# The difference of two probabilities, in two tiles of four added up in PSUM by products with the identity

## The reference, cut to what matters

```python
def _prob(x):
    x = jnp.tanh(x) * 0.499 + 0.5
    return jnp.clip(x / (jnp.sum(x, axis=-1, keepdims=True) + EPS), EPS)
q_prob = _prob(q)
k_prob = _prob(k)
log_ratio = jnp.log(q_prob) - jnp.log(k_prob)
sid = jnp.einsum('bnd,bmd->bnm', q_prob - k_prob, log_ratio)
attn = jax.nn.softmax(-sid / D ** 0.5, axis=-1)
attn_feat = jnp.einsum('bnm,bmd->bnd', attn, v)
```

## Time and profile before

| | |
|---|---|
| median of 3 runs | 262.26 us (262.22 to 262.55) |
| the profiled execution | 262.99 us, span of its instructions 261.1 us |
| mean granted clock of TensorE | 0.933 |
| stage two | about 64 to 124 us of the span |
| busy over the span | VectorE 225.0 us, ScalarE 216.2, TensorE 209.4, GpSimd 188.9 |

### The profile page before, as it was taken

How to read it: one execution, slowest core, us unless ns; L and a number is a source line. 1 busy time by engine, 2 the same in 40 slices (tenths; PEclk the granted TensorE clock), 3 DMA queues, 4 the chain that set the end, 5 groups by cost and what they waited for, 6 DMA issues and landing times.

```text
span 261.1 us, 5925 instructions
## 1 busy us (share of the span) xinstructions
PE 209.4 (80%) x1723; PEld 176.3 (68%) x1723; DVE 225.0 (86%) x843; ACT 216.2 (83%) x774; POOL 188.9 (72%) x250
## 2 busy tenths in 40 slices
PE   2676676754499888887899999999999999996711
PEld 1664554533387666666689988888889888895600
DVE  2899999988879999999525889999999999999892
ACT  4599999998889999989997888988898887776521
POOL 2477666764899999991885796969697888666552
PEclk9999999795569999999999999999999999999765
DMA  5667554540000000000328189897978888977922
GB/s 140 188 201 204 158 154 135 154 113 1 1 0 3 0 3 3 1 3 4 40 32 91 12 100 135 122 133 110 151 115 132 129 125 128 137 121 121 103 61 61
DMA packets 51360, 23.65 MB, mean 91 GB/s; under 512 B 9856, under 2 KB 51200, under 8 KB 51328
## 3 DMA queue, kind: packets, MB, share of 16 engines
q0 software_dynamic: 15856, 7.87, 28.0%
q1 hardware_dynamic: 35040, 15.21, 21.9%
q10 hardware_dynamic: 432, 0.20, 0.4%
HBM read 9.37 MB, written 4.19 MB: 52 GB/s over the span
## 4 chain that ended last, share of the span: by engine, by line
POOL 28%; DVE 23%; ACT 20%; issue 13%; PE 11%; DMA 3%; SPq 0%; POOLq 0%; DVEq 0%; ACTq 0%
POOL F L407 7%; POOL xrstd L448 7%; ACT TQK L523 6%; ACT TQK L507 6%; POOL orstd L442 6%; DVE q_c L810 5%; POOL F L454 5%; DVE LN_c L818 5%; DVE F L838 5%; PE bank L1011 3%; ACT PV L518 3%; DMA LN_c<-in_ctx_dram 3%; ACT vT_c L512 2%; PE bank L960 1%; DVE F L863 1%
## 5 line engine op out<-in xcount | busy, mean ns | idle before, releaser
L1011 PE MATMUL bank<-W2T,TQK 128*128 128x128 f32 x512 | 68.7, 282 | 2.6 <-ACT TQK L545 2.5
L1011 PEld LDWEIGHTS bank<-W2T,TQK 128*128 128x128 f32 x512 | 64.0, 194 | 8.5 <-ACT TQK L545 4.0
L545 ACT ACTIVATE TQK<-bank,b1c 128x512 f32<-128x512 f32 (+1 forms) x68 | 44.5, 661 | 10.7 <-PE bank L1004 10.4
L448 POOL TENSOR_TENSOR xrstd<-xvar,pow_c 128x4 f32<-128x4 f32 (+1 forms) x17 | 18.5, 1090 | 23.2 <-DVE xvar L726 23.2
L362 POOL TENSOR_TENSOR xrstd<-xvar,pow_c 128x4 f32<-128x4 f32 x16 | 16.8, 1051 | 21.5 <-DVE xvar L726 21.5
L1002 PE MATMUL bank<-hTh,W1h 128*128 128x512 f32 (+1 forms) x68 | 30.4, 447 | 0.8 <-DVE hTl L801 0.8
L407 POOL DMA_DIRECT2D F<-rows x17 | 26.0, 1529 | 5.6 <-DVE E_c L796 5.6
L1003 PE MATMUL bank<-hTl,W1h 128*128 128x512 f32 (+1 forms) x68 | 26.1, 384 | 0.0
L1004 PE MATMUL bank<-hTh,W1l 128*128 128x512 f32 (+1 forms) x68 | 25.9, 382 | 0.0
L960 PE MATMUL bank<-WdT,vT_c 128*128 128x128 f32 x128 | 20.5, 309 | 4.8 <-ACT vT_c L512 4.6
L951 PE MATMUL bank<-ident,LN_c 128*128 128x128 f32 x64 | 12.3, 322 | 13.9 <-DMA LN_c<-in_ctx_dram 13.9
(11 more groups left out here) (129 smaller groups left out, 645.2 us busy)
## 6 DMA issues: line engine op xcount, KB each, us to landing
F<-rows POOLq DMA_DIRECT2D x29, 256.0 KB, 4.7
LN_c<-in_ctx_dram SPq DMA_DIRECT2D x16, 256.0 KB, 3.0
X<-in_x_dram SPq DMA_DIRECT2D x16, 256.0 KB, 3.3
out_dram<-F SPq DMA_DIRECT2D x15, 256.0 KB, 2.3
LN_c<-in_L_xattn_W_dram SPq DMA_DIRECT2D x1, 256.0 KB, 3.5
lT_c<-in_L_xattn_W_dram SPq DMA_DIRECT2D x1, 256.0 KB, 3.7
F<-rows POOLq DMA_DIRECT2D x2, 128.0 KB, 4.8
out_dram<-F SPq DMA_DIRECT2D x2, 128.0 KB, 1.8
```

The lines of the kernel that those rows point to most:

```text
L448: pool.tensor_tensor(buf(xrstd, x1, G), buf(xvar, x1, G), pow_c[:, 0:x1.g], ALU.pow).then_inc(x1_rstd, 1)
L545: act.activation(hid(m, j), m1_bank(m, j), ACT.Gelu, bias=b1c[:, j:j + 1]).then_inc(gelu_ready, 1)
L1011: last = pe.matmul(M2_B[m.buf][:, i * D:(i + 1) * D], hid(m, j)[:, i * D:(i + 1) * D], W2T[:, j * D:(j + 1) * D], start=(j == 0 and i == 0 ...
```

## The change

GpSimd makes k's part for all tiles of a piece and nothing else in this stage. ScalarE no longer makes k's parts; for the first half of a piece's tiles it scales q's tanh by GAINQ in place in TQ, after Ln has read it (`qparts`, behind Exp in the step). TensorE adds the two parts of those tiles in PSUM while it transposes them: a product of k's part with the identity, and a product of q's part with the identity accumulated onto it. VectorE makes the difference for the other half as before, and the log ratio for all tiles. D now waits for three semaphores: k's parts, q's parts, VectorE's differences. The waits on `kpart_act`, `diff_pool` and `lr_pool` are gone.

```diff
@@ gpsimd phase2
-                    for i in range(by_act(k), k.g):
-                        last = pool.tensor_scalar(tile(diff_c, k, i), all_tile(TK, k, i), per_tile(GAINK, k, i),
+                    for i in range(k.g):
+                        last = pool.tensor_scalar(tile(k_c, k, i), all_tile(TK, k, i), per_tile(GAINK, k, i),
                                                   per_tile(SHIFT, k, i), ALU.mult, ALU.add)
                     last.then_inc(kpart, 1)
-                    if k.g == G:
-                        i = G - 1
...
-                        pool.tensor_scalar(qpart_c, all_tile(TQ, k, i), per_tile(GAINQ, k, i), None,
-                                           ALU.mult).then_inc(qpart, 1)
...
-                        pool.tensor_tensor(tile(diff_c, k, i), qpart_c, tile(diff_c, k, i),
-                                           ALU.add).then_inc(diff_pool, 1)
...
-                        pool.tensor_scalar(ln_tile(0, k, i), ln_tile(0, k, i), per_tile(LRATIO, k, i), None,
-                                           ALU.add).then_inc(lnq_pool, 1)
...
-                        pool.tensor_tensor(ln_tile(1, k, i), ln_tile(0, k, i), ln_tile(1, k, i),
-                                           ALU.subtract).then_inc(lr_pool, 1)
@@ scalar
-            def kparts(k):
-                wait(act, dT_ps, k.n - 1)
-                if is_piece(k, NORMS):
-                    act.wait_ge(norms, 2)
+            def qparts(k):
+                act.wait_ge(ln_ready, k.n + 1)
                 for i in range(by_act(k)):
-                    last = act.activation(tile(diff_c, k, i), all_tile(TK, k, i), ACT.Identity,
-                                          bias=per_tile(SHIFT, k, i), scale=per_tile(GAINK, k, i))
-                last.then_inc(kpart_act, 1)
+                    last = act.activation(all_tile(TQ, k, i), all_tile(TQ, k, i), ACT.Copy, scale=per_tile(GAINQ, k, i))
+                last.then_inc(q_act, 1)
@@ scalar phase2, behind Exp
+                k0 = at(0)
+                if k0.live:
+                    if k0.n == 0:
+                        act.wait_ge(norms, 1)
+                    if k0.n == NORMS:
+                        act.wait_ge(norms, 2)
+                    qparts(k0)
@@ scalar phase2, behind the copies
-                k = at(-1)
-                if k.live:
-                    kparts(k)
@@ vector phase2
-                    for i in range(by_dve(k)):
-                        last = dve.scalar_tensor_tensor(out=tile(diff_c, k, i), in0=all_tile(TQ, k, i),
...
-                    last.then_inc(diff_ready, 1)
+                    for i in range(by_act(k), k.g):
+                        last = dve.scalar_tensor_tensor(out=tile(k_c, k, i), in0=all_tile(TQ, k, i),
...
+                    last.then_inc(diff_dve, 1)
...
-                    for i in range(by_dve(k)):
+                    for i in range(k.g):
                         last = dve.scalar_tensor_tensor(out=ln_tile(1, k, i), in0=ln_tile(0, k, i),
@@ tensor phase2
-                    pe.wait_ge(diff_ready, k.n + 1)
-                    pe.wait_ge(diff_pool, wholes(k.n + 1))
+                    pe.wait_ge(kpart, k.n + 1)
+                    pe.wait_ge(q_act, k.n + 1)
+                    pe.wait_ge(diff_dve, k.n + 1)
                     wait(pe, dT_sb, k.n)
-                    for i in range(k.g):
-                        last = pe.transpose(D_B[:, i * D:(i + 1) * D], tile(diff_c, k, i), ident[:, :])
+                    for i in range(by_act(k)):
+                        at_i = D_B[:, i * D:(i + 1) * D]
+                        pe.matmul(at_i, tile(k_c, k, i), ident[:, :], start=True, stop=False)
+                        pe.matmul(at_i, all_tile(TQ, k, i), ident[:, :], start=False, stop=True)
+                    for i in range(by_act(k), k.g):
+                        last = pe.transpose(D_B[:, i * D:(i + 1) * D], tile(k_c, k, i), ident[:, :])
```

More of the change, by code:

```diff
@@ L152, in xattn_ffn_kernel @@
         vT_c = sb("vT_c", [P, 2 * C])
-        diff_c, dT_c = q_c, vT_c
+        k_c, dT_c = q_c, vT_c
         lT_c = sb("lT_c", [P, 2 * C])
@@ L174, in xattn_ffn_kernel @@
         r16_c = LN_c[:, 2 * C:3 * C].bitcast(F16)
-        qpart_c = RNORM[:, :]
         Wd_raw = E_c[:, 0:D]
@@ L199, in by_act @@
             return k.g // 2
[L201 to L205, removed]
         def tile(t, k, i):
@@ L274, in xattn_ffn_kernel @@
         norm_step, halfk_ready, norms, lratio = sem("norm_step"), sem("halfk_ready"), sem("norms"), sem("lratio")
-        kpart, kpart_act, ln_ready, diff_ready, lr_ready = (
-            sem("kpart"), sem("kpart_act"), sem("ln_ready"), sem("diff_ready"), sem("lr_ready"))
-        qpart, diff_pool, lnq_pool, lr_pool = sem("qpart"), sem("diff_pool"), sem("lnq_pool"), sem("lr_pool")
+        kpart, ln_ready, q_act, diff_dve, lr_ready = (
+            sem("kpart"), sem("ln_ready"), sem("q_act"), sem("diff_dve"), sem("lr_ready"))
         dT_ps, dT_sb, lT_ps, lT_sb = sem("dT_ps"), sem("dT_sb"), sem("lT_ps"), sem("lT_sb")
@@ L378, in phase2 @@
                         pool.wait_ge(norms, 2)
-                    for i in range(by_act(k), k.g):
-                        last = pool.tensor_scalar(tile(diff_c, k, i), all_tile(TK, k, i), per_tile(GAINK, k, i),
+                    for i in range(k.g):
+                        last = pool.tensor_scalar(tile(k_c, k, i), all_tile(TK, k, i), per_tile(GAINK, k, i),
                                                   per_tile(SHIFT, k, i), ALU.mult, ALU.add)
                     last.then_inc(kpart, 1)
-                    if k.g == G:
-                        i = G - 1
-                        pool.wait_ge(kpart, k.n + 1)
-                        if is_piece(k, 0):
-                            pool.wait_ge(norms, 2)
-                        pool.tensor_scalar(qpart_c, all_tile(TQ, k, i), per_tile(GAINQ, k, i), None,
-                                           ALU.mult).then_inc(qpart, 1)
-                        pool.wait_ge(qpart, k.n + 1)
-                        pool.tensor_tensor(tile(diff_c, k, i), qpart_c, tile(diff_c, k, i),
-                                           ALU.add).then_inc(diff_pool, 1)
-                        pool.wait_ge(ln_ready, k.n + 1)
-                        if is_piece(k, 0):
-                            pool.wait_ge(lratio, 1)
-                        pool.tensor_scalar(ln_tile(0, k, i), ln_tile(0, k, i), per_tile(LRATIO, k, i), None,
-                                           ALU.add).then_inc(lnq_pool, 1)
-                        pool.wait_ge(lnq_pool, k.n + 1)
-                        pool.tensor_tensor(ln_tile(1, k, i), ln_tile(0, k, i), ln_tile(1, k, i),
-                                           ALU.subtract).then_inc(lr_pool, 1)
             pool.wait_ge(norms, 1)
@@ L566, in phase2 @@
                     wait(act, lr_ready, k.n - 1)
-                    wait(act, lr_pool, wholes(k.n - 1))
                     wait(act, lT_ps, k.n - 1)
@@ L615, in _ @@
             act.wait_ge(sel_ready, 1)
-            act.wait_ge(norms, 1)
-            kparts(pairs[0])
             run_steps(pairs, 2, phase2)
@@ L806, in phase2 @@
                 if k.live:
-                    dve.wait_ge(kpart_act, k.n + 1)
                     dve.wait_ge(kpart, k.n + 1)
-                    for i in range(by_dve(k)):
-                        last = dve.scalar_tensor_tensor(out=tile(diff_c, k, i), in0=all_tile(TQ, k, i),
-                                                        scalar=per_tile(GAINQ, k, i),
-                                                        in1=tile(diff_c, k, i), op0=ALU.mult, op1=ALU.add)
-                    last.then_inc(diff_ready, 1)
+                    for i in range(by_act(k), k.g):
+                        last = dve.scalar_tensor_tensor(out=tile(k_c, k, i), in0=all_tile(TQ, k, i),
+                                                        scalar=per_tile(GAINQ, k, i), in1=tile(k_c, k, i),
+                                                        op0=ALU.mult, op1=ALU.add)
+                    last.then_inc(diff_dve, 1)
                     dve.wait_ge(ln_ready, k.n + 1)
@@ L1051, in phase2 @@
                 if k.live:
-                    pe.wait_ge(diff_ready, k.n + 1)
-                    pe.wait_ge(diff_pool, wholes(k.n + 1))
+                    pe.wait_ge(kpart, k.n + 1)
+                    pe.wait_ge(q_act, k.n + 1)
+                    pe.wait_ge(diff_dve, k.n + 1)
                     wait(pe, dT_sb, k.n)
-                    for i in range(k.g):
-                        last = pe.transpose(D_B[:, i * D:(i + 1) * D], tile(diff_c, k, i), ident[:, :])
+                    for i in range(by_act(k)):
[4 more added lines that the diff above has]
+                        last = pe.transpose(D_B[:, i * D:(i + 1) * D], tile(k_c, k, i), ident[:, :])
                     last.then_inc(dT_ps, 1)
                     pe.wait_ge(lr_ready, k.n + 1)
-                    pe.wait_ge(lr_pool, wholes(k.n + 1))
                     wait(pe, lT_sb, k.n)
```

## The result

The changed kernel takes 264.25 us at the median of 18 executions, the kernel before 262.74 in as many (its first three, which the prediction had, were at 262.26). The ratio is 1.0054 with a 95% interval of 1.0035 to 1.0072: slower by 1.4 us, or by 1.5 between the medians. The forecast was a loss of 0.48, to 262.7, with a range that ended at 264.1.

A forecast was written before the change was run, and what follows sets the result against it. VectorE bounds stage two at 3.44 us a step; afterwards TensorE at 3.27. Twelve steps gain 1.18, the start loses 1.66: +0.48 on the 262.26 median gives 262.7, range 261.1 to 264.1.

The forecast's parts named there:

- D's price: TensorE's group D in stage two: ten records after the change, 1.09 us against 0.49 before, upper bound 1.22.
- a sign of being wrong: Check on D's length in the profile after: the prediction is wrong if D takes over 1.15 or under 1.0.
- rival 1: TensorE's mixed group slower, 0.122 for each record: step 3.40, +2.1 us, time 264.3; chance 0.15.
- The start-up sum: First pieces of stage two: added records at the lower clock make EP(1) begin at 78.95 instead of 77.29, loss 1.66.
- the late rise: Start of stage two: TensorE's clock assumed to rise at about 75.8, after D(0) and D(1) at the lower level.
- rival 3: Clock rises sooner, under D(1) at about 72.4: EP(1) at 77.3 as today, time 261.1; chance 0.17.
- VectorE's relief: VectorE in stage two: most of 0.56 us waiting inside its instructions goes, step 3.44 to about 3.05.
- rival 2: VectorE stays held up by GpSimd at 3.44 a step: +1.1 us, time 263.4; chance 0.11.
- the mechanism that I called a lock: VectorE and GpSimd get in each other's way on two-SBUF-input instructions, 0.56 us of VectorE's step.
- ScalarE, GpSimd and the tail: ScalarE busy stays 3.16, scalings 0.77 for 0.77; GpSimd 2.1 of a step, hidden; tail net nothing.
- the shift is carried whole: Rest of the kernel after EP(13): the +0.48 us there passes undiminished to the end.

The follow-up runs named there:

- changed, lower group: Changed kernel unaltered, the faster of two groups of execution times: nine of the first 18 from 262.71 to 263.58 us; profiled execution 262.81.
- changed, upper group: Changed kernel unaltered, the slower of two groups of execution times: nine of the first 18 from 264.91 to 265.46 us; profiled execution, from a rerun, 264.92.
- twelve products ahead: Changed kernel plus twelve unused identity products on TensorE between stage one and stage two: median 261.87 us, ratio 0.9978.
- first two pieces as before: Changed kernel, but in pieces 0 and 1 VectorE makes all four differences and no tile is added up in PSUM: median 263.56 us, ratio 1.0044.
- nothing in PSUM: Changed kernel with VectorE making all four differences and GpSimd still all k's parts: median 264.44 us, ratio 1.0064.
- one tile: Changed kernel with one tile of four instead of two added up in PSUM, VectorE making three differences: median 261.71 us, ratio 0.9957.
- one tile, first pieces, products: Changed kernel with one tile of four in PSUM, none in pieces 0 and 1, and twelve unused identity products before stage two: median 258.60 us, ratio 0.9870.

## Why the prediction was wrong

Its own frame can be laid over all the profiles: when EP(1) begins, how long to EP(13), and what is left of the span.

| profile | EP(1) | EP(13) | mean step | span | span less EP(13) |
|---|---|---|---|---|---|
| before | 77.29 | 117.71 | 3.37 | 261.1 | 143.4 |
| changed, lower group | 76.90 | 117.60 | 3.39 | 261.0 | 143.4 |
| changed, upper group | 78.88 | 119.58 | 3.39 | 263.0 | 143.4 |
| twelve products ahead | 76.84 | 117.54 | 3.39 | 261.0 | 143.5 |
| first two pieces as before | 77.85 | 118.56 | 3.39 | 262.0 | 143.4 |
| nothing in PSUM | 77.40 | 119.37 | 3.50 | 262.8 | 143.4 |
| one tile | 78.42 | 116.45 | 3.17 | 259.8 | 143.4 |
| one tile, first pieces, products | 75.44 | 113.46 | 3.17 | 256.8 | 143.3 |

**The step that failed is D's price.** I took 1.09 for its ten records, and it is 1.21, past the 1.15 that I had named as a sign of being wrong. All ten records, transposes and products alike, cost 0.111, and the first of the group 0.10 more. That 0.10 is most of the miss; I had no term for it beside products. It stands behind S, whose records are narrower (128x64), and is absent in the one profile where D(0) follows products of its own shape: 0.22 for the first two records there, 0.32 here. (The 0.49 of the old D was 0.44 and 0.05.) The rest is the products' price, 0.04 over what I took for eight of them, less 0.02 for two transposes that I had priced too high. The eight L960 at 0.101 were the best row of their kind. Of the eleven such groups between 16 and 60 us of that trace with the clock at its upper level throughout, the ten others take 0.91 or 0.92, 0.114 a record. So TensorE's step is 2.67 + 0.72 = 3.39, not 3.27: rival 1, which I had at 3.40 and 0.15. Over twelve steps the 0.12 is 1.44 us, three times the whole forecast.

**The start-up sum was right, as one of two cases.** Forecast for the late rise: D(0) 67.4, S(0) 71.4, EP(0) 75.65, EP(1) 78.95. Measured in the upper group: 67.24, 71.35, 75.49, 78.88. That it agrees to a tenth is in part luck: D costs 0.1 more than I took at either level, and the rise at 75.2 instead of 75.8 gives it back. The lower level's 0.214 a record came from a row of stage one in which the profile shows no granted clock under 1.00; in D(0) of the changed kernel, at a granted 0.50, two records take 0.43, so the price holds. In the profile of the lower group the clock rises early instead, as in rival 3, and EP(1) begins 0.4 earlier than before the change; by its times that group is half of the executions. I treated the moment of the rise as one fact to be guessed; it varies over the executions of one kernel, and the time is a mixture. By EP(1) and the 0.28 that the twelve steps lose, the late case comes to 1.59 + 0.28 = +1.9 and the early one to -0.39 + 0.28 = -0.1, which is what the two spans show against 261.1. By the times, the groups' medians lie 2.5 and 0.4 over the 262.74 of the kernel before, 0.6 and 0.5 more than that. It is a matter of which executions were profiled: the one of the kernel before was 0.25 above its median, the two of the changed kernel 0.3 and 0.4 below their groups'. What sets the moment of the rise no run shows; two profiles of one kernel have it at 70.2 and at 75.2.

Whether products in place of transposes helped the early rise, as rival 3 had it, is not shown, but the profiles point that way. With transposes alone in D(0) and D(1), and no added work that raised the clock by itself, the rise came at 73.8 to 75.8 in all seven; with products in them, at 70.0, 70.2, 75.2 and 75.6. In all four TensorE also has more records in D(0) and D(1), so that products and longer work are not told apart. The nearest pair has the same twelve products ahead: the clock fell at 66.6 and at 67.0, and rose at 70.0 in the changed kernel and at 73.8 in the kernel before. Each is a single profile of something that varies. In the kernel before, too, products stand ahead of the rise at 75.8: EP(0), from 73.64, and the start of S(1).

**VectorE's relief was right.** 3.05 forecast, 3.00 measured, and rival 2, VectorE held at 3.44, is out. No run shows the mechanism that I called a lock. Of the cause the runs show this much: undisturbed, a two-input instruction of VectorE costs 0.26; with nothing in PSUM, one L372 under the first of four added 0.19; a TENSOR_TENSOR together with the end of a k part added 0.20 to 0.40 in three successive steps; without the two TENSOR_TENSOR, VectorE's cost 0.26 to 0.28 each; under four L832, which read PSUM, nothing was added (1.04). So one-input instructions can cost VectorE something too, but in the changed kernel they hardly do: of the four L372 from 96.99 the first ones lie under L789, which is at 0.27 each, and the four take 2.20, against 1.74 where VectorE idled.

**ScalarE, GpSimd and the tail** came out as said, with two scalings at 0.58 instead of 0.77. That the shift is carried whole is the table's last column: 143.3 to 143.5 in eight profiles, and in the other five of the experiments too.

So the change does trade VectorE's 3.44 for TensorE's 3.39. That gains 0.05 in each of the ten later steps. But in the first two TensorE had been ahead of VectorE before, at 2.94 and 3.10, and these now take 3.39 as well, which loses 0.37 a step. Together EP(1) to EP(13) takes 40.70 instead of 40.42, where I had forecast 39.24. What remains is the start, dearer by 1.6 when the clock rises late.

## What to carry to other kernels

When work moves off the engine that sets the pace, price the receiving engine's whole step from several rows like the new mix, not from the best row, and count what the group costs where it follows another shape. With twelve equal steps, a tenth of a microsecond turned the steady part from a gain of 1.2 into a loss of 0.3. Move only as much as levels the two: one tile gave -0.4% where two gave +0.5%. And where TensorE becomes the pace right behind an idle stretch, look at the level of its clock there, profile more than one execution, and keep the first pieces light.

## What the runs showed of the hardware that was not expected

In one program the granted clock rose from 0.50 to 1.00 at 70.2 in one profiled execution and at 75.2 in another; the same work then took 3.39 a step in both, and the span differed by 2.0 us. Within one measurement on one chip the times fell into both groups. For the kernel before, whose times show no two groups, no run shows an early rise, so how much of it VectorE would hide stays open.

Where VectorE ran two-input instructions back to back, GpSimd was the one that took longer: with nothing in PSUM, beside eight of them from 69.43, four L372 took 3.42 us, against 1.74 where VectorE idled (with one tile, at 74.53), and VectorE lost nothing visible. In the steady stretch with nothing in PSUM the same four took 1.83 and VectorE lost 0.19.
